# Attention products of a fused layer as three one-pass products of high and low parts, in place of plain f32 products

## The reference, cut to what matters

```
q, k, v = layernorm(x) @ wq.T, ctx @ wk.T, ctx @ wv.T          # 16 heads of 16
x  = x  + tanh(g_xattn[0]) * (softmax(q k.T / 16) v) @ wo.T
x  = x  + tanh(g_ffn[0])   * ffn0(layernorm(x))                # ternary weights, relu squared, low-rank term
D  = sqrt(|a|^2 + |b|^2 - 2 a @ b.T)   # a = ctx, b = layernorm(x); then a dynamic time warping path
x  = x  + tanh(g_xattn[1]) * align(ctx, path(D))
x  = x  + tanh(g_ffn[1])   * ffn1(layernorm(x))                # quantised, gelu
```

## Time and profile before

| what | value |
|---|---|
| median of 3 runs | 1828.75 us (1828.48 to 1829.92) |
| the profiled execution, device time | 1828.01 us |
| its span, first to last instruction | 1826.2 us |
| attention phase, at its steady pace | from about 100 us to about 1000 us |
| one iteration there | 32.93 us |

### The profile page before, as it was taken

One profiled execution on the slowest core, in us unless ns is written; L12 is line 12 of the kernel. 1 busy time (PEld: TensorE's weight loads), 2 busy tenths in 40 slices (PEclk: granted clock), 3 DMA queues, 4 the chain that ended last, 5 costly groups with the idle time before them and its releaser, 6 DMA issues. The chain is left out here.

```text
span 1826.2 us, 35776 instructions
## 1 busy us (share of the span) xinstructions
PE 1414.0 (77%) x10821; PEld 1072.6 (59%) x10821; DVE 1420.9 (78%) x4062; ACT 1107.6 (61%) x2395; POOL 551.6 (30%) x998
## 2 busy tenths in 40 slices
PE   5899999999999999999999986133332004899896
PEld 4578788888887888878888765000001002566664
DVE  6677777777777777777777642899998998999996
ACT  3476676676766767667677662243335002999997
POOL 3122222322222223222233221200000002778785
PEclk8899999999999999999999997555555555999999
DMA  5444445444444444444543310322220002222321
GB/s 175 139 129 116 138 125 146 121 116 140 124 135 124 117 142 130 118 129 123 147 123 107 111 42 18 99 59 61 60 45 11 0 0 81 76 87 92 100 76 47
DMA packets 322936, 179.49 MB, mean 98 GB/s; under 512 B 93793, under 2 KB 318193, under 8 KB 322802
## 3 DMA queue, kind: packets, MB, share of 16 engines
q1 hardware_dynamic: 322802, 178.07, 35.0%
HBM read 122.91 MB, written 50.33 MB: 95 GB/s over the span
## 5 line engine op out<-in xcount | busy, mean ns | idle before, releaser
L982 DVE TENSOR_REDUCE nmax<-s 128x2 f32<-128x512 f32 x512 | 327.0, 681 | 7.9 <-PE s L454 6.9
L709 ACT ACTIVATE pt<-s 128x512 f32<-128x512 f32 x512 | 281.0, 611 | 70.0 <-PE s L471 69.9
L1074 POOL TENSOR_TENSOR r<-rl 128x512 f32<-128x512 f32 x128 | 133.1, 1040 | 328.4 <-ACT rl L739 285.6
L454 PE MATMUL s<-kst,qst 96*128 96x256 bf16 x1024 | 158.2, 275 | 11.6 <-DVE nmax L982 8.0
L471 PE MATMUL s<-qst,kst 128*128 128x256 bf16 x1024 | 156.9, 275 | 1.1 <-ACT pt L709 0.8
L1341 PE MATMUL gate<-diag,one 128*128 128x512 f16 x35 | 21.3, 608 | 171.7 <-DVE left L1432 171.7
L739 ACT ACTIVATE rl<-wb,fscl 128x256 f32<-128x256 f32 x256 | 107.8, 476 | 64.7 <-PE wb L555 64.7
L551 PE MATMUL wb<-x2l,wfcT 128*128 128x256 f32 x512 | 143.3, 302 | 0.7 <-ACT dd L761 0.7
L485 PE MATMUL oacc<-pt,vw 128*32 128x256 f32 x2048 | 137.0, 385 | 6.4 <-ACT pt L709 6.0
L951 DVE TENSOR_TENSOR r2l<-r,r2h 128x512 fp32r<-128x512 f32 x128 | 88.6, 692 | 65.2 <-POOL r L1074 40.3
L418 PE MATMUL wb<-wprT,r2l 128*128 128x256 f32 x512 | 131.8, 296 | 6.9 <-DVE r2l L951 6.9
(11 more groups left out here) (270 smaller groups left out, 3951.9 us busy)
## 6 DMA issues: line engine op xcount, KB each, us to landing
kst<-k_parts_dram SPq DMA_DIRECT2D x384, 64.0 KB, 2.5
qst<-q_parts_dram SPq DMA_DIRECT2D x384, 64.0 KB, 2.4
k_parts_dram<-kp SPq DMA_DIRECT2D x32, 384.0 KB, 5.2
q_parts_dram<-qp SPq DMA_DIRECT2D x32, 384.0 KB, 3.1
xin<-in_x_dram SPq DMA_DIRECT2D x32, 256.0 KB, 2.8
cT<-in_ctx_T_dram SPq DMA_DIRECT2D x32, 256.0 KB, 2.7
xres<-in_x_dram SPq DMA_DIRECT2D x32, 256.0 KB, 3.1
cin<-in_ctx_dram SPq DMA_DIRECT2D x32, 256.0 KB, 4.6
```

What stands on the lines that cost most here:

```text
L454: last = pe.matmul(s1[h % 2][:, t, :], qst[b.p][0:MAXROW, h, t * P:t * P + P], kst[b.p][0:MAXROW, h, :], start=True, stop=True)
L709: act.activation(pt[h % (2 * HPG)][:], s2[h % 2][:], ACT.Exp).then_inc(e["expd"], 1)
L982: v.tensor_reduce(nmax[:, T * h:T * h + T], s1[h % 2][:], AX.X, ALU.max, negate=True)\
L1074: pool.tensor_tensor(r2[:], rl[:, k % 2], rl[:, k % 2], ALU.mult)\
```

## The change

Every operand of the five products gets a high and a low part in float32r, and each of the 20 plain products of a batch becomes three float32r matmuls: high by low, low by high, high by high. The parts are made as follows.

- The weights: four copies on ScalarE and four subtractions on VectorE, once, ahead of iteration -2. The raw weights are loaded into tiles that are free at that time.
- xT, onT and yT: the copy on ScalarE out of PSUM stays and gives the high part; a subtraction on VectorE (x_low, on_low, y_low) gives the low part. The PSUM buffer is released by the subtraction, not by the copy.
- cT and cD: the DMA goes into one raw tile each (`cT_raw`, `cD_raw`) in place of two alternating tiles; a copy on ScalarE (ctx_high, products_high) and a subtraction on GpSimd (ctx_low, products_low) make the parts. The loads wait for the subtraction of the batch before, no longer for TensorE.

Some tiles are laid over others to make room, and a counter that nobody reads is dropped.

```diff
+            def three(bank, lhs, rhs, c, block):
+                pe.matmul(bank, lhs[0][:, c, block], rhs[1][:, c, :], start=(c == 0), stop=False)
+                pe.matmul(bank, lhs[1][:, c, block], rhs[0][:, c, :], start=False, stop=False)
+                return pe.matmul(bank, lhs[0][:, c, block], rhs[0][:, c, :], start=False, stop=(c == C - 1))
...
             def load_ctx_turned(b):
-                w("v_mm", b.n - 1)
-                sp.dma_start(cT[b.p][:], ct_d[b.n].rearrange(feat, p=P)).then_inc(cT_in[b.p], 16)
+                w("c_low", b.n)
+                sp.dma_start(cT_raw[:], ct_d[b.n].rearrange(feat, p=P)).then_inc(e["cT_in"], 16)
             def load_ctx_products(b):
-                w("ab_mm", b.n - 1)
-                sp.dma_start(cD[b.p][:], ct_d[b.n].rearrange(feat, p=P)).then_inc(cD_in[b.p], 16)
+                w("d_low", b.n)
+                sp.dma_start(cD_raw[:], ct_d[b.n].rearrange(feat, p=P)).then_inc(e["cD_in"], 16)
...
             def proj(b, t):
...
-                    w("xT_cp", b.n + 5), w("max_split", b.n + 3)
+                    w("x_low", b.n + 5), w("max_split", b.n + 3)
...
             def turn_half(b):
-                w("halves", b.n + 1), w("x1_res", b.n + 2), w("yT_cp", b.n + 1), w("low_low", b.n + 1)
+                w("halves", b.n + 1), w("x1_res", b.n + 2), w("y_low", b.n + 1), w("low_low", b.n + 1)
...
+            def weights_high():
+                act.wait_ge(e["w_straight"], 64)
+                for n, (high, low) in (("wk", wkT), ("wq", wqT), ("wv", wvT), ("wo", woT)):
+                    act.activation(high[:], straight[n], ACT.Copy).then_inc(e["w_act"], 1)
+            def ctx_high(b):
+                w("cT_in", 16 * (b.n + 1), 16 * NB)
+                w("v_mm", b.n - 1)
+                act.activation(cT[b.p][0][:], cT_raw[:], ACT.Copy).then_inc(e["c_high"], 1)
+            def products_high(b):
+                w("cD_in", 16 * (b.n + 1), 16 * NB)
+                w("ab_mm", b.n - 1)
+                act.activation(cD[b.p][0][:], cD_raw[:], ACT.Copy).then_inc(e["d_high"], 1)
...
                 if there(i):
                     exps(i, 0, 4)
+                if there(z):
+                    products_high(z)
...
                 if there(i):
                     copy_group(i, 1)
+                if there(ct):
+                    ctx_high(ct)
                 if there(y):
                     distance(y)
...
+            def x_low(b):
+                w("xT_cp", b.n + 1)
+                v.tensor_tensor(xT[1][:], B_TURN_X[:], xT[0][:], ALU.subtract).then_inc(e["x_low"], 1)
...
                 if there(a):
+                    x_low(a)
                     k_remainder(a)
...
                 if there(s):
                     maxima(s, 2, 4)
+                if there(z):
+                    on_low(z)
...
                 if there(nx):
                     ln1(nx)
+                if there(y):
+                    y_low(y)
                 if there(z):
                     low_half(z)
...
+            def products_low(b):
+                w("d_high", b.n + 1)
+                high, low = cD[b.p]
+                pool.tensor_tensor(low[:], cD_raw[:], high[:], ALU.subtract).then_inc(e["d_low"], 1)
...
                 if there(a):
                     parts(a, "k_parts", kr, kp)
+                if there(z):
+                    products_low(z)
                 rstd(i)
                 if there(y):
                     halves(y)
                 if there(a):
                     parts(a, "q_parts", qr, qp)
+                if there(ct):
+                    ctx_low(ct)
```

More of the change, by code:

```diff
@@ L66, in off, with done @@
         return Batch(self.half + k // 2, k % 2)
-def done(eng, sem, count, most, tick=None):
+def done(eng, sem, count, most):
     if isinstance(count, int):
@@ L115, in sem @@
             return ctx.enter_context(nc.semaphore(name))
-        wqT, wkT, wvT, woT = (sb(n, [P, C, D]) for n in ("wqT", "wkT", "wvT", "woT"))
+        wqT, wkT, wvT, woT = ([sb(n + part, [P, C, D], F32R) for part in "hl"] for n in ("wqT", "wkT", "wvT", "woT"))
         wfcT, fscl = sb("wfcT", [P, C, F], F32R), sb("fscl", [P, FT])
@@ L128, in attention_phase @@
         xres = [sb(f"xres{p}", [P, T, D]) for p in range(2)]
-        xhat, xT = sb("xhat", [P, T, D]), sb("xT", [P, C, S])
-        cT = [sb(f"cT{p}", [P, C, S]) for p in range(2)]
-        cD = [sb(f"cD{p}", [P, C, S]) for p in range(2)]
+        xhat, xT = sb("xhat", [P, T, D]), [sb(f"xT{part}", [P, C, S], F32R) for part in "hl"]
+        cT = [[sb(f"cT{part}{p}", [P, C, S], F32R) for part in "hl"] for p in range(2)]
+        cT_raw, cD_raw = sb("cT_raw", [P, C, S]), sb("cD_raw", [P, C, S])
+        cD = [[sb(f"cD{part}{p}", [P, C, S], F32R) for part in "hl"] for p in range(2)]
         qp, kp = sb("qp", [P, 3, C, S], BF16), sb("kp", [P, 3, C, S], BF16)
@@ L138, in attention_phase @@
         nsp = sb("nsp", [2 * NH, 2, P], BF16)
-        pt = [sb(f"pt{r}", [P, T, S]) for r in range(2 * HPG)]
+        pts = sb("pts", [P, 2 * HPG, T, S])
+        pt = [pts[:, r] for r in range(2 * HPG)]
         osb = sb("osb", [P, NG, S])
-        rs, on, onT = sb("rs", [P, T, NH // 2]), sb("on", [P, T, D]), sb("onT", [P, C, S])
+        rs, on = sb("rs", [P, T, NH // 2]), sb("on", [P, T, D])
+        onT = [sb(f"onT{part}", [P, C, S], F32R) for part in "hl"]
         x1 = [sb(f"x1_{p}", [P, T, D]) for p in range(2)]
@@ L149, in attention_phase @@
         x2 = sb("x2", [P, T, D])
-        yn, yT = sb("yn", [P, T, D]), sb("yT", [P, C, S])
+        yn, yT = sb("yn", [P, T, D]), [sb(f"yT{part}", [P, C, S], F32R) for part in "hl"]
         half, hpart, hrows = sb("half", [P, T]), sb("hpart", [P, 4, 32]), sb("hrows", [P, S], BF16)
@@ L178, in attention_phase @@
                  "fc_mm", "pr_mm", "y_t", "half_t", "ab_mm", "s1_mm", "s2_mm", "av_mm",
-                 "xT_cp", "qh_cp", "kh_cp", "vw_cp", "onT_cp", "x2T_cp", "x2_low", "low_mm", "low_cp", "low_low", "relu", "expd", "o_cp", "yT_cp", "half_cp",
+                 "xT_cp", "x_low", "on_low", "y_low", "c_high", "c_low", "d_high", "d_low", "cT_in", "cD_in", "qh_cp", "kh_cp", "vw_cp", "onT_cp", "x2T_cp", "x2_low", "low_mm", "low_cp", "low_low", "relu", "expd", "o_cp", "yT_cp", "half_cp",
                  "dist", "aa_sum",
@@ L238, in w @@
             def w(s, count, most=NB):
-                done(sp, e[s] if isinstance(s, str) else s, count, most, e["sp_tick"])
+                done(sp, e[s] if isinstance(s, str) else s, count, most)
             def load_x(b):
@@ L424, in out_proj @@
             def out_proj(b):
-                w("onT_cp", b.n + 1)
+                if at(b, 0):
+                    pe.wait_ge(e["w_made"], WO_LOW)
+                w("on_low", b.n + 1)
                 w("kh_cp", b.n + 4), w("k_rem", b.n + 4), w("relu", 4 * b.n, 4 * NB)
[L427 to L431, removed]
+                project(B_OUT, onT, woT, "wo_mm")
             def queries(b):
-                w("xT_cp", b.n + 1)
-                w("onT_cp", b.n - 2), w("qh_cp", b.n), w("q_rem", b.n)
+                if at(b, 0):
+                    pe.wait_ge(e["w_made"], WQ_LOW)
+                w("x_low", b.n + 1)
+                w("on_low", b.n - 2), w("qh_cp", b.n), w("q_rem", b.n)
                 project(B_QUERIES, wqT, xT, "q_mm")
@@ L439, in values_proj @@
                 w("x2_res", b.n - 2)
[L440 to L445, removed]
+                if at(b, 0):
+                    pe.wait_ge(e["w_made"], WV_LOW)
+                w("c_low", b.n + 1)
+                project(B_VALUES, cT[b.p], wvT, "v_mm")
             def scores1(b, lo, hi):
@@ L910, in apply_norm, with weights_straight, on_low, y_low @@
                 last.then_inc(e[s], 1)
+            def weights_straight():
+                for k, (n, (high, low)) in enumerate((("wk", wkT), ("wq", wqT), ("wv", wvT), ("wo", woT))):
+                    v.wait_ge(e["w_act"], STRAIGHT_HIGH + k + 1)
+                    v.tensor_tensor(low[:], straight[n], high[:], ALU.subtract).then_inc(e["w_made"], 1)
+            def x_low(b):
+                w("xT_cp", b.n + 1)
+                v.tensor_tensor(xT[1][:], B_TURN_X[:], xT[0][:], ALU.subtract).then_inc(e["x_low"], 1)
+            def on_low(b):
+                w("onT_cp", b.n + 1)
+                v.tensor_tensor(onT[1][:], B_TURN_ON[:], onT[0][:], ALU.subtract).then_inc(e["on_low"], 1)
+            def y_low(b):
+                w("yT_cp", b.n + 1)
+                v.tensor_tensor(yT[1][:], B_TURN_Y[:], yT[0][:], ALU.subtract).then_inc(e["y_low"], 1)
             def x_stats(b):
@@ L1063, in w @@
             def w(s, count, most=NB):
-                done(pool, e[s], count, most, e["pool_tick"])
+                done(pool, e[s], count, most)
             def parts(b, made, r, pt_):
```

76 lines of the change are left out of this document (42 added, 34 removed).

## The result

| | median, us | runs |
|---|---|---|
| before | 1828.62 | 4, 1827.05 to 1829.92 |
| changed | 1851.79 | 4, 1847.39 to 1855.42 |

The ratio is 1.0126, with a 95% interval of 1.0101 to 1.0151: the change makes the kernel 23 us slower, where 1823 and a gain were forecast. 1851.8 lies above the range, 1800 to 1845, too. The profiled execution of the changed kernel took 1855.4 us, with a span of 1853.2, 27.0 more than before.

The account below looks back on a forecast made before the run. TensorE was taken to bound the kernel at 32.93 us an iteration. 1828.0 - 8.7 (29 iterations at -0.30) + 3 for filling and emptying = 1822.3, with 0.7 for the median of runs 1823; range 1800 to 1845.

Parts of the forecast that it names:

- What bounds the kernel, and what TensorE saves: TensorE sets the pace of 32.93 us an iteration; five product groups save it 1.58, about 0.32 each.
- the full 1.58 an iteration: Rival: TensorE's whole saving shows in each iteration, 1783 us in all; chance 0.03.
- Who is late next: At turn_y and turn_xh2, TensorE waits for yn and xh: load of cD, copy and subtraction start `ln_y` 0.46 us later.
- The rival in which the subtraction does not hold up `ln_y`: cD lands early, VectorE's chain sets yn's shift at -0.2 us, the kernel takes 1804; chance 0.15.
- D: The shift of yn, ahead of turn_y, against the kernel before: forecast +0.46 us, or -0.2 from VectorE's chain alone.
- D - 0.76: Change of one iteration: yn's shift less the gain up to low_rank behind the shorter products, -0.30 us.
- What that leaves: From yn on: turn_half moves by yn's shift less 0.44 us, low_rank by it less 0.76; the iteration changes by -0.30.
- filling and emptying: Pipeline's start and end: +1.2 to 1.4 before keys(0), +1 in first iterations, +1 in last two; together +3 us.
- the likeliest case: `ln_y` waits for GpSimd's subtraction, an iteration changes by -0.30 us; 1823, own range 1814 to 1831; chance 0.53.
- the slower side: Rival: the load of cT delays that of cD by 0.73 us, an iteration costs +0.43, the kernel 1844; chance 0.29.

Follow-up runs that it names:

- e1: The changed kernel with products_high moved behind exps(8:10) on ScalarE and products_low behind ctx_low on GpSimd; 1812.1 us.
- e3: The changed kernel with the load of cD issued earlier by SP, behind the first half of the stack loads of the iteration before; 1813.6 us.
- e7: The changed kernel with 14 extra, unused bf16 matmuls of 128 columns on TensorE ahead of its wait at turn_y; 1840.0 us.

## Why the prediction was wrong

*What bounds the kernel, and what TensorE saves*: right in the main. Twelve matmuls of a group follow each other at 0.115 to 0.12 us (the first step is often 0.20 to 0.22), in e1 the iteration did fall, and the full 1.58 an iteration was nowhere to be had, since VectorE's chain stands in the way.

*Who is late next*: right in each link. What stands beside them was priced at nothing: ScalarE's copies and the clock (3 and 4 below). The load is issued 8.5 us after max_rows, lands 4.8 later, the copy takes 0.63, `ln_y` follows GpSimd's subtraction, and TensorE waits at turn_y for yn. The rival in which the subtraction does not hold up `ln_y` came out when it was built: e1 and e3 stand at 1812 and 1814, where its sum gave 1804.

The step that failed is the term of -0.30 us an iteration, D - 0.76: the size of this chain and of what is gained behind it. It was wrong at four places.

1. *The price of the subtraction on GpSimd.* I took 1.10 between bounds of 1.04 and 1.16. It is 1.29 in the changed kernel and 1.27 in e1, where it runs at another time, so this is the price of the kind (two f32 inputs in SBUF, float32r out) and not of a collision there. Both my rows had other operands: one read the same tensor twice and wrote f32, one had a bf16 input and output. The true value lay outside my bounds. 0.19 an iteration.
2. *What that leaves.* I put yn's shift D at +0.46; the median yn is 16.85 after max_rows against 16.14, so +0.71, of which 0.19 is the price above and 0.03 the held `ln_v` (`ln_y` starts 0.11 behind the subtraction and not 0.08). From there I counted a gain of 0.76 against D. Up to low_rank it is 0.46. turn_half starts 3.07 after yn (408.40 to 405.33) against 3.37 before, 0.30 sooner and not 0.44, as an idle TensorE takes up work 0.2 after `hpart` and not 0.06. The products group saves 0.16 and not 0.32: its first matmul and the switches to and from `hrows` are not at 0.117. So D - 0.76 = -0.30 becomes +0.71 - 0.46 = +0.25. With the mean D of the 19 late iterations (+0.75) it is +0.29, and their one stretch of half clock adds some 0.07: the measured +0.35. In e1, without the chain, yn comes 16.01 after max_rows, D is -0.13 (I had -0.2), and -0.13 - 0.46 is the measured 32.34 against 32.93. That is also why e1 and e3 stay above the 1804 of the rival.
3. *A median in place of a distribution.* Landings of `cD` up to 6.4 us are in the trace of before as well, between 100 and 400 us; I looked at it from 400 us on only the earlier trace rows. Before, they cost nothing. In the changed kernel the two longest, 6.3 and 7.3, are in that stretch and make the copy start 14.9 and 15.8 after max_rows. Two more loads there are issued late, 9.9 and 9.7 after max_rows (9.9 before the change too), and start the copy at 14.9 and 14.4. In the late ones ScalarE's five steps behind the load also come too late for TensorE (1.82 us at 235.04), which I had named and priced at nothing.
4. *The clock.* That the new waits could let the granted clock fall stands nowhere in the prediction. The earlier trace rows showed 1.00, and I treated it as given. Filling the wait gave 12 us in e7, of which 5 to 6 are the clock by the estimate there. It may also be why the changed kernel's runs scatter by 8 us, against 3 for those of before and for e7's; that was not tested.

The forecast of 1823 used these steps: -8.7 for 29 iterations at -0.30, +3 for filling and emptying. The 27 iterations after the third max_rows gave 12.3 + 6.6 = +18.9 instead. Filling cost 4.8 where I had 2.2; in e1, without the chain, it cost 1.7. The last two iterations and the end cost 3.3 where I had about 1. (The upper end of the likeliest case is 1832 by its own bounds, not 1831; nothing hangs on it.) The decision point that I gave for the slower side, a landing 13.5 us after max_rows, was near: the median copy started at 13.3 to 13.4. So small errors in size decided the sign, and a range that ended at 1845 left no room for what a wait can set off.

One statement was wrong in fact and would have led further. I wrote that nobody needed `cD` until products, 6 us later. The batch z whose `cD` is loaded in an iteration is batch y of the next, so products needs it a whole iteration later. The new copy and subtraction had 39 us of room; e1 uses it.

## What to carry to other kernels

When TensorE sets the pace with 0.2 to 0.4 us of slack at a wait, a new step that stands in an in-order list ahead of the step that feeds this wait is on the path, however idle its engine is on average; look up when its result is first needed, and put it right before that, behind everything that others wait for. Price such a chain with the late landings in it and not with the median, and from a row with the same operand kinds. A TensorE that has begun to stand idle may also lose its clock, as it did here behind some of the waits of 1.3 us: check the granted clock by windows, not over the span.

## What the runs showed of the hardware that was not expected

GpSimd's f32 subtraction of two different SBUF tiles of 128x512 into float32r takes 1.27 to 1.30 us, against 1.04 where both inputs are the same f32 tile and the output is f32.

A small VectorE instruction can be held up by it. `ln_v`, a tensor_scalar on 128x6 elements, takes 0.17 in e1 and e3. In the changed kernel, where GpSimd's subtraction is under way when it starts, it takes up to 1.17 and ends 0.03 behind the subtraction (403.89 and 403.86 in the rows above). The changed kernel, then e1:

```profile
L1068 DVE TENSOR_SCALAR ln_v<-ln_mv x15: 171/818/1172, 403.0 to 867.6; 128x6 f32<-128x6 f32 x15
```
```profile
L1068 DVE TENSOR_SCALAR ln_v<-ln_mv x15: 170/172/173, 416.1 to 868.9; 128x6 f32<-128x6 f32 x15
```

The Trainium skill, "SBUF — State Buffer", the section "Who interferes with whom", says that VectorE (in some of its modes, or with two SBUF inputs) and GpSimd take the same ports under an exclusive lock, and that the later one is blocked until the other is done. The trace agrees on the blocking, in 10 of the 15 iterations from 400 to 900 us; `ln_v` has one SBUF input, and in which mode it ran no run here shows. It cost some 0.15 us where it happened: `ln_y` then starts 0.11 after the subtraction's end, and in the iterations in which `ln_v` was done before 0.04 ahead of that end as the profile gives it.

Useless matmuls can make a kernel faster: 14 of them in each iteration, 0.8 us of work in a wait of 1.1 to 1.3, kept the clock at the level of 2.4 GHz, and the kernel became 12 us faster, 5 to 6 of them by the clock itself as estimated under e7.
